# Windowed-attention layers: engine programs reordered, and exponentials taken head by head with the negated maximum as bias

## The reference

```python
for i in range(DEPTH):          # DEPTH = 6, 16 heads of 64, window 32
    x = attn_layer(shift_tokens(x), Wqkv[i], q_scale[i], k_scale[i], Wo[i]) + x
    x = ffn_layer(shift_tokens(x), ln_g[i], ln_b[i], W1[i], b1[i], W2[i], b2[i]) + x
# attn_layer: q, k, v = x @ Wqkv; q, k = l2norm * scale; rotary;
#   sim = q k^T * 8 over the own and the previous window, masked; softmax(sim) @ v; @ Wo
# ffn_layer: a, gate = split(layernorm(x) @ W1 + b1); a * gelu(gate) @ W2 + b2
```

## Time and profile before

| | us |
|---|---|
| median of three runs | 3662.96 |
| profiled execution | 3655.01 |
| its span, first to last instruction | 3653.2 |
| PE busy | 3035.9 (83%) |
| DVE busy | 2316.2 (63%) |
| ACT busy | 1468.4 (40%) |
| POOL busy | 1495.5 (41%) |

### The profile page before, as it was taken

The page is one execution under the profiler, slowest core; times in us unless marked ns, Lnnn a source line. Parts: engine busy times, 40 slices in busy tenths (PEclk is TensorE's granted clock), DMA queues, the critical chain, the costliest instruction groups (busy, mean ns, idle before and its releaser), DMA issues. The chain is left out here.

```text
span 3653.2 us, 94645 instructions
## 1 busy us (share of the span) xinstructions
PE 3035.9 (83%) x39263; PEld 2166.0 (59%) x39263; DVE 2316.2 (63%) x4318; ACT 1468.4 (40%) x2454; POOL 1495.5 (41%) x1462
## 2 busy tenths in 40 slices
PE   4769999999759888888888888888888859888876
PEld 1168888888736555555555555555555535555544
DVE  6832222222149888888888888888888833655622
ACT  3522222222225455555545545545555514444420
POOL 0043333333137556555655555555555502222100
PEclk9977777777769999999999999999999978999975
DMA  0000000000022112212121121121111100000000
GB/s 26 0 6 0 0 0 0 0 0 0 14 92 55 44 37 57 62 48 57 48 62 47 47 73 41 53 54 56 44 45 36 46 27 1 0 0 0 0 9 12
DMA packets 60542, 109.42 MB, mean 30 GB/s; under 512 B 14466, under 2 KB 18580, under 8 KB 59300
## 3 DMA queue, kind: packets, MB, share of 16 engines
q1 hardware_dynamic: 59668, 103.40, 10.2%
q10 hardware_dynamic: 528, 1.05, 0.1%
HBM read 29.43 MB, written 1.05 MB: 8 GB/s over the span
## 5 line engine op out<-in xcount | busy, mean ns | idle before, releaser
L1551 POOL TENSOR_TENSOR l_rot_a<-l_rot_a,l_rot_b 128x512 f32<-128x512 f32 x384 | 487.5, 1271 | 461.6 <-DVE l_rot_b L1366 459.7
L1560 POOL TENSOR_TENSOR l_qk<-l_rot_a,l_rn 128x512 f32<-128x512 f32 x384 | 391.3, 1049 | 235.3 <-DVEq L1407 235.3
L1022 PE MATMUL l_A<-l_wts,l_H 128*128 128x512 f32 x768 | 411.8, 625 | 29.6 <-ACT l_H L1310 21.3
L1360 DVE TENSOR_TENSOR l_rot_a<-l_A,l_tab 128x512 f32<-128x512 f32 x384 | 263.7, 687 | 167.4 <-ACT l_sq L1244 164.0
L1244 ACT ACTIVATE l_sq<-l_A 128x512 f32<-128x512 f32 x384 | 232.0, 604 | 333.1 <-PE l_A L1022 333.1
L1112 PE MATMUL l_T<-ident,l_qk 128*128 128x128 f32 x1536 | 220.3, 287 | 59.7 <-ACT l_qT L1275 59.6
L1366 DVE TENSOR_TENSOR l_rot_b<-l_A,l_tab 128x512 f32<-128x512 f32 x384 | 261.1, 680 | 0.0
L1370 DVE TENSOR_REDUCE l_ss<-l_sq 128x8 f32<-128x512 f32 x384 | 259.3, 675 | 0.0
L1097 PE MATMUL l_O<-l_pT,l_vw 64*64 64x32 f32 x9216 | 198.8, 220 | 72.6 <-ACT l_pT L1250 70.9
L1112 PEld LDWEIGHTS l_T<-ident,l_qk 128*128 128x128 f32 x1536 | 170.6, 145 | 142.3 <-issue 131.8
L1097 PEld LDWEIGHTS l_O<-l_pT,l_vw 64*64 64x64 f32 x9216 | 187.9, 135 | 95.6 <-ACT l_pT L1250 93.6
(11 more groups left out here) (353 smaller groups left out, 6667.6 us busy)
## 6 DMA issues: line engine op xcount, KB each, us to landing
l_vw<-l_vn SPq DMA_DIRECT2D x384, 128.0 KB
l_vw<-l_vn SPq DMA_DIRECT2D x360, 64.0 KB
l_wts<-in_l_wts SPq DMA_DIRECT2D x18, 650.0 KB, 5.1
l_tab<-in_l_tables SPq DMA_DIRECT2D x6, 1024.0 KB, 5.3
l_wts<-in_l_wts SPq DMA_DIRECT2D x6, 635.5 KB, 4.8
a_mask<-in_a_mask SPq DMA_DIRECT2D x1, 1024.0 KB
result<-x SPq DMA_DIRECT2D x1, 1024.0 KB, 5.1
d_w_qkv<-in_d_w_qkv SPq DMA_DIRECT2D x1, 864.0 KB, 4.4
```

What stands on the lines that cost most here:

```text
L1022: pe.matmul(A[j % 2][:], cols(m), w_of(m)[:, C_QKV + 512 * j:C_QKV + 512 * j + 512], start=True, stop=True).then_inc(pq_done, 1)
L1360: dve.tensor_tensor(rot_a[p][:, j, :].rearrange("p (a d) -> p a d", d=DH), src.rearrange("p (a d) -> p a d", d=DH), table[:, a, t:t + 1, : ...
L1551: pool.tensor_tensor(rot_a[m % 2][:, j, :], rot_a[m % 2][:, j, :], rot_b[:, j, :], ALU.add).then_inc(rot_rdy, 1)
L1560: pool.tensor_tensor(qk[:, j, :].rearrange("p (a d) -> p a d", d=DH), rot_a[p][:, j, :].rearrange("p (a d) -> p a d", d=DH), rn[p][:, 8 * ...
```

## The change

In the attention: `soft_shift` keeps the maximum, now negated by the instruction, and loses the subtraction. `exps` reads the scores from `S` and writes `sd`, with one instruction for each of the 16 heads and that head's negated maximum as the bias. `masks` waits for the exponentials instead of the subtraction.

In the feed-forward part: `normed` moves from DVE to ACT as scale and bias, four instructions at the end of the kind 1 slot; DVE computes the bias (`l_shift`) in one small instruction.

In the orders: on PE `turn_norm` goes from the head of its slot to behind `scores`, `narrow` to behind `masks`, and `turn_probs` 1 before `project(n+2, 2)`; ACT follows. On DVE `feed_back` goes behind rope 1, and `add_back` goes before `inverse_roots`. The first step of `inverse_roots` takes a constant instead of the tile `half`.

```diff
--- before.py
+++ after.py
...
@@ -1034,3 +1035,3 @@
             def masks(m):
-                pe.wait_ge(sd_rdy, m)
+                pe.wait_ge(e_rdy, m)
                 for e in range(2):
@@ -1182,4 +1183,2 @@
             for n in range(FIRST_SLOT, LAST_SLOT + 1):
-                if group_at(n, 2) is not None:
-                    turn_norm(n, group_at(n, 2))
                 if group_at(n, 3) is not None:
@@ -1190,4 +1189,2 @@
                     linears(k, 0)
-                if group_at(n, 4) is not None:
-                    narrow(group_at(n, 4))
                 if has(n + 2):
@@ -1196,5 +1193,11 @@
                     masks(n)
+                if group_at(n, 4) is not None:
+                    narrow(group_at(n, 4))
+                if has(n):
                     scores(n, range(HP))
+                if group_at(n, 2) is not None:
+                    turn_norm(n, group_at(n, 2))
                 if has(n - 1):
                     turn_probs(n - 1, 0)
+                    turn_probs(n - 1, 1)
                 if has(n + 2):
@@ -1202,3 +1205,2 @@
                 if has(n - 1):
-                    turn_probs(n - 1, 1)
                     values(n - 1)
@@ -1252,4 +1254,8 @@
             def exps(m):
-                act.wait_ge(sd_rdy, m + 1)
-                act.activation(sd[m % 2][:], sd[m % 2][:], ACT.Exp).then_inc(e_rdy, 1)
+                act.wait_ge(mx_rdy, m + 1)
+                if m >= 2:
+                    act.wait_ge(p_rdy, m - 1)
+                for a in range(HEADS):
+                    last = act.activation(sd[m % 2][:, a, :], S[:, a, :], ACT.Exp, bias=mx[:, a:a + 1])
+                last.then_inc(e_rdy, 1)
 
@@ -1296,2 +1302,10 @@
 
+            def normed(n, k):
+                act.wait_ge(shift_rdy, k + 1)
+                act.wait_ge(xnT_done, k)
+                for i in range(GT):
+                    c = 2 * HEADS + i
+                    last = act.activation(xn[:, i, :], xt[:, i, :], ACT.Identity, scale=rn[n % 2][:, c:c + 1], bias=shift[:, i:i + 1])
+                last.then_inc(xn_rdy, 1)
+
             def gelu(k, i):
@@ -1311,2 +1325,6 @@
             for n in range(FIRST_SLOT, LAST_SLOT + 1):
+                if group_at(n, 3) is not None:
+                    gelu(group_at(n, 3), 2)
+                if has(n + 2):
+                    square(n + 2, 1)
                 if group_at(n, 2) is not None:
@@ -1316,12 +1334,7 @@
                     keep_norm(k)
-                if group_at(n, 3) is not None:
-                    gelu(group_at(n, 3), 2)
-                if has(n + 2):
-                    square(n + 2, 1)
                 if has(n - 1):
                     keep_pT(n - 1, 0)
+                    keep_pT(n - 1, 1)
                 if has(n + 2):
                     square(n + 2, 2)
-                if has(n - 1):
-                    keep_pT(n - 1, 1)
                 if has(n):
@@ -1346,2 +1359,4 @@
                     square(n + 3, 0)
+                if group_at(n, 1) is not None:
+                    normed(n, group_at(n, 1))
 
@@ -1374,8 +1389,4 @@
                 dve.wait_ge(s_done, m + 1)
-                dve.tensor_reduce(mx[:], S[:], AX, ALU.max).then_inc(mx_rdy, 1)
-                dve.wait_ge(mx_rdy, m + 1)
-                if m >= 2:
-                    dve.wait_ge(p_rdy, m - 1)
-                dve.tensor_tensor(sd[m % 2][:], S[:], mx[:].rearrange("p (a o) -> p a o", o=1).to_broadcast([P, HEADS, 2 * WIN]),
-                                  ALU.subtract).then_inc(sd_rdy, 1)
+                dve.wait_ge(e_rdy, m)
+                dve.tensor_reduce(mx[:], S[:], AX, ALU.max, negate=True).then_inc(mx_rdy, 1)
 
@@ -1399,4 +1410,6 @@
                     dve.wait_ge(qk_rdy, 4 * (m - 2) + 4)
+                if group_at(n - 2, 1) is not None:
+                    dve.wait_ge(xn_rdy, group_at(n - 2, 1) + 1)
                 dve.wait_ge(ss_rdy, 4 * m + 4)
-                step(dve.scalar_tensor_tensor(low, low, 1e-24, half[:], ALU.max, ALU.mult), 1)
+                step(dve.tensor_scalar(low, low, 1e-24, -0.5, ALU.max, ALU.mult), 1)
                 step(dve.scalar_tensor_tensor(y.bitcast(I32), low.bitcast(I32), -0.5, magic[:], ALU.mult, ALU.add), 2)
@@ -1420,2 +1433,3 @@
                 dve.wait_ge(st_rdy, GT * k + GT)
+                dve.wait_ge(xn_rdy, k)
                 for i in range(GT):
@@ -1451,7 +1465,3 @@
                 r = rn[n % 2][:, 2 * HEADS:]
-                dve.wait_ge(xnT_done, k)
-                for i in range(GT):
-                    last = dve.scalar_tensor_tensor(xn[:, i, :], xt[:, i, :], mv[:, i, 0:1], r[:, i:i + 1].to_broadcast([P, D]),
-                                                    ALU.subtract, ALU.mult)
-                last.then_inc(xn_rdy, 1)
+                dve.scalar_tensor_tensor(shift[:], mv[:, :, 0], -1.0, r, ALU.mult, ALU.mult).then_inc(shift_rdy, 1)
 
@@ -1517,6 +1526,6 @@
                     product(group_at(n, 3), 0)
-                if group_at(n, 4) is not None:
-                    feed_back(group_at(n, 4))
                 if has(n + 2):
                     rope(n + 2, 1)
+                if group_at(n, 4) is not None:
+                    feed_back(group_at(n, 4))
                 if has(n):
@@ -1529,5 +1538,8 @@
                     rope(n + 2, 3)
+                if has(n - 1):
+                    add_back(n - 1)
+                if has(n + 2):
                     if group_at(n, 1) is not None:
                         dve.wait_ge(var_rdy, group_at(n, 1) + 1)
-                    inverse_roots(n + 2)
+                    inverse_roots(n, n + 2)
                 elif group_at(n, 1) is not None:
@@ -1535,4 +1547,2 @@
                     lone_roots(group_at(n, 1))
-                if has(n - 1):
-                    add_back(n - 1)
                 if group_at(n, 1) is not None:
```

More of the change, by code:

```diff
@@ L887, in local_layers @@
         rn_t = sb("l_rn_t", [P, RN])
-        half = sb("l_half", [P, RN])
         magic = sb("l_magic", [P, RN])
@@ L905, in local_layers @@
         mv = sb("l_mv", [P, GT, 2])
+        shift = sb("l_shift", [P, GT])
         xn = sb("l_xn", [P, GT, D])
@@ L926, in local_layers @@
             "rn_step", "rn_rdy", "qk_rdy", "qkT_done", "qkT_rdy", "kc_rdy"))
-        s_done, mx_rdy, sd_rdy, e_rdy, rs_sum, rs_rdy, p_rdy = (sem("l_" + s) for s in (
-            "s_done", "mx_rdy", "sd_rdy", "e_rdy", "rs_sum", "rs_rdy", "p_rdy"))
+        s_done, mx_rdy, e_rdy, rs_sum, rs_rdy, p_rdy = (sem("l_" + s) for s in (
+            "s_done", "mx_rdy", "e_rdy", "rs_sum", "rs_rdy", "p_rdy"))
         v_done, v_rdy, vw_rdy = (sem("l_" + s) for s in ("v_done", "v_rdy", "vw_rdy"))
@@ L935, in local_layers @@
             "g_done", "gl_rdy", "a_done", "u_rdy", "f_done", "f_rdy", "edge_rdy", "side_rdy"))
+        shift_rdy = sem("l_shift_rdy")
         back_done, back_rdy = sem("l_back_done"), sem("l_back_rdy")
@@ L1388, in sums, with inverse_roots @@
                 dve.reciprocal(rs[:], rs[:]).then_inc(rs_rdy, 1)
-            def inverse_roots(m):
+            def inverse_roots(n, m):
                 low, y, t, base = ss[m % 2][:], rn[m % 2][:], rn_t[:], NEWTON * m
@@ L1495, in _ @@
                 dve.memset(ss[p][:], 1.0)
-            dve.memset(half[:], -0.5)
             dve.memset(magic[:], float(0x5F3759DF - (1 << 30) - (1 << 22)))
@@ L1517, in _ @@
                     product(group_at(n, 3), 0)
+                if has(n + 2):
+                    rope(n + 2, 1)
                 if group_at(n, 4) is not None:
                     feed_back(group_at(n, 4))
-                if has(n + 2):
-                    rope(n + 2, 1)
                 if has(n):
```

## The result

The changed kernel takes 3826.76 us, the median of four runs (3822.58 to 3830.05), against 3665.11 for the kernel before, the median of four runs beside it (with 3662.96 as the median of its first three): a ratio of 1.0435 (95% interval 1.0404 to 1.0466). It is slower, as forecast, and 37 us above the predicted 3790, inside the range of 3695 to 3860. The profiled span grew from 3653.2 to 3820.8 us.

The account below looks back on a forecast made before the run. A loop through DVE, ACT and PE was taken to bound the kernel. 22.5 periods lose 110 us and the first five steps 20: 3655 + 130 = 3785, stated as 3790, range 3695 to 3860.

Parts of the forecast that it names:

- The loop: DVE-ACT-PE chain from one end of `output` (y) to the next: four-slot period of 79.8 us at full clock, from 77.5.
- The sixteen exponentials: On ACT, sixteen 64-column instructions replace one of 1024 columns: 3.42 us from first start to last end, not 1.06.
- `add_back` first: On DVE, `add_back` and then the roots follow the end of `output`: rope 0 starts 3.31 us after it, not 2.01.
- `normed` on ACT: 3.70 us leave DVE, `l_shift` takes 0.8 there; four ACT instructions take 1.5 in all; PE's wait for `l_xn` stays under 2.
- PE's waits for `l_qT`: PE, before `turn_qk` 2, waits 4.8, 2.2, 3.1 and 1.8 us in slot kinds 1, 2, 3 and 0.
- The waits of DVE: DVE waits about 1.6 us at `sums` in most slots and near 1.9 at `add_back` in each slot.
- y to the start of the exponentials: From the end of `output` to the exponentials' start: 9.8, 9.3, 10.9 and 11.4 us in kinds 1, 2, 3, 0.
- The clock: Half clock on PE behind its `l_qT` wait: 2.2 times a period at 1.6 us each, 3.5 in all, making 83.3.
- DVE's load: Rival, 0.07: DVE's busy time sets the pace and falls 7.8 us a period, so the kernel gets faster, 3475 us.
- The quiet clock: Rival, 0.16: PE's clock doesn't fall more often, so the kernel takes 3698 to 3706 us.
- The serial case: Rival, 0.09: small exponentials on ACT don't overlap and take 4.96 us a slot; 146 us on top, 3935.
- No change: Rival, 0.06: an exponential's fixed part is near 0.1 us, not 0.154; a period is 78.2 with kind 1's half clock.

Follow-up runs that it names:

- e3: The changed kernel with `add_back` behind `inverse_roots` again, all else kept: 3663.68 us, 0.9996 of the kernel before.
- e2: The kernel before with only the sixteen exponentials with bias, without the subtraction; orders and `normed` as before: 3791.88 us, 1.0353 of the kernel before.
- e4: The changed kernel with 1 to 4 unused projections on PE in front of `turn_qk` 2: 3733.84 us, 1.0182 of the kernel before.
- e5: The changed kernel with the subtraction and single exponential back and `add_back` behind `inverse_roots`: 3502.34 us, 0.9541 of the kernel before.
- e8: e5 with `project_v` on PE in front of `turn_qk` 2 and 3: 3495.74 us, 0.9528 of the kernel before.

## Why the prediction was right, and where it was short

Point by point, by the prediction's own steps:

- **The loop.** It holds. At full clock the four kinds take 19.9, 19.3, 20.5 and 21.1 us after the change (each mean slot less what its last piece exceeds 4.76, without the last slot of the stack), together 80.8, where 19.4, 18.9, 20.5 and 21.0, together 79.8, were predicted.
- **The sixteen exponentials.** 3.42 predicted, 3.38 measured. The single instruction is longer than thought, 365 ns at the median instead of 310, and the overlap larger by as much: (3.38 - 0.37) / 15 is 0.20 from start to start. The estimate from the Trainium skill's page "ScalarE: Activation LUTs", section "What ACT_TABLE_LOAD costs", was 3.93; the measurement decides. A single one is longer here than the 333 ns that the Trainium skill's figures there make for 64 columns, an estimate from that page, and the overlap is larger than its 93 ns (365 less 200), so that the row of sixteen is cheaper.

```profile
L1259 ACT ACTIVATE l_sd<-l_S,l_mx x1536: 305/365/438, 1089.6 to 3101.8; 128x64 f32<-128x64 f32 x192
```

- **`add_back` first.** Rope 0 starts 3.39 after y, predicted 3.31; e3 shows that this place is worth 163 us in the changed kernel.
- **`normed` on ACT.** The four took 478 ns each, predicted 460; `l_shift` 1.05, predicted 0.8. The wait of PE for `l_xn` was predicted under 2 us and is 2.5 on average (59.8 in 24); the roots, which `l_shift` needs, now start only after y. This is one of the prediction's own signs of being right that failed.
- **PE's waits for `l_qT`.** Predicted 4.8, 2.2, 3.1 and 1.8 in kinds 1, 2, 3 and 0; the timeline of PE has 4.9, 1.7, 2.8 and 1.4 on average.
- **The waits of DVE.** `sums` was to wait about 1.6 and waits 1.9 on average (184.0 in 96). `add_back` was to wait near 1.9 in each slot and waits 3.2 (303.1 in 96). The half clock in front of y, 1.1 us a slot on average, is part of this; the parts were not split.
- **y to the start of the exponentials**, the first undersized term: predicted 9.8, 9.3, 10.9 and 11.4, measured 10.3, 9.7, 10.9 and 11.5. Most of it is in kind 1, and it is a misreading rather than a new cost. The prediction took rope 0 to the maximum, 5.14, from the one slot of the earlier trace rows. That was a short one: over the kernel before the mean of this stretch is 5.75, and after the change it is 5.67. The last step of `moments`, four columns, took 0.32 in that slot (first row) and over 1.2 in ten others of the 24 (second row: the shortest, the median and the longest in ns). Over the four kinds this term is 1.0 a period.

```profile
1653.58 0.32 DVE L1424 TENSOR_SCALAR l_ss<-l_mv 128x4 f32<-128x4 f32 x1
...
L1424 DVE TENSOR_SCALAR l_ss<-l_mv x24: 171/427/1252, 1181.0 to 2961.9; 128x4 f32<-128x4 f32 x24
```

- **The clock**, the second: "2.2 x 1.6 = 3.5" a period, measured 2.4 + 1.1 + 1.0 + 0 = 4.5 in kinds 1, 2, 3, 0 (6.4 being the fall in every slot). In kind 1 the half clock covers `turn_qk` and `project_v` and costs 2.4, not 1.6. In kind 2, 14 of 21 slots pay, not 0.4 of them: there a wait of 1.7 follows PE's wait for `l_xn` in the same slot, 2.2 to 2.4 in each of these, and the prediction counted each wait alone. The 14 that pay waited 1.4 to 2.0 for `l_qT`; of the 7 others six waited 1.0 to 1.2. In e3, where PE waits for `l_xn` in only one of these slots, none of 22 waits of 1.1 to 2.0 at this place costs anything. This speaks for the two waits acting together, but only one of e3's waits is as long as the 2.0 of most that pay, and no run changes one wait alone. Kind 3 has fewer, 9 of 20 instead of 0.7, at about 2.2 each.

The two terms make 2.0 of a period. Over the stack it is 1.8 (85.1 against 83.3), as that last kind 1 slot is 3 us shorter. Times 22.5 periods these are 40 us, less 2 us over the first five steps (17.9 measured, 20 predicted; the first took 15.5, the others 19.4 to 20.4 where 19.4 was predicted). That is the miss in the profiled execution: 168 measured, 130 predicted. The mechanism held piece by piece, so the direction was no luck. The size of the clock's term rests on few slots: the share of slots that fall to half clock was counted on 15 waits, and came out higher in kind 2 and lower in kind 3.

- **The rivals.** DVE's load is refuted: DVE has 242 us less to do and the program is slower; the freed time is in front of `sums` (184.0 us) and `add_back` (303.1). The Trainium skill's page "Perfetto Trace Analysis", section "Optimizing Scalar/DVE Operations", proposes moving work from a saturated DVE to Scalar; e2 moves the subtraction that way from a DVE that is busy for 86% of a period, and costs 3.5%. Whether 86% is saturated that page of the Trainium skill doesn't say; here the busy share didn't decide it. The quiet clock is refuted by the clock itself, and e4 measures what it would have given: at least 93 us. The serial case is out by its 3.38 us. "No change" would have needed a fixed part near 0.1 us an instruction; 0.15 stands.

What the prediction didn't see is how much the rest of the change is worth. It had one number for the whole of kind 2; e5 shows that the other orders with `normed` on ACT take 163 us off, and that the two losing parts put 324 on top.

## What to carry to other kernels

Where two engines are each 86% busy, add up one round between them: if the pieces make the whole period, an instruction counts for its length between waits and not for its load, and work taken off a busy engine is lost if it lengthens the chain. A step that waits for the end of a round (here `add_back`) goes behind everything that the next round needs, however short it is. And a wait on PE is priced twice, as time and as clock: look at every wait with the ones just before it. Unused work in the gap gave 93 us back here (e4); useful work moved into it only moved the gap (e8), so count what the moved matmul itself waits for.

## What the runs showed of the hardware

- **Padding paid.** Ten unused 512-column matmuls a period made the program 2.4% faster (3733.84 against 3826.76), because PE behind them ran at 2.4 GHz and not at 1.2: the granted clock from 1300 to 2700 us rose from 0.93 to 0.98.
- **A short wait can cost the clock.** Waits of up to 1.6 us at `turn_qk` 2 left the clock full in kind 0 (none of 22 slots took over 0.2 us longer); in kind 2, behind another wait of 2.2 to 2.4 us, 14 of 21 waits did cost it, all of them 1.4 to 2.0 long. Waits of 2.5 to 3.0 in kind 3 cost it in 9 of 20, and waits of 4.2 to 5.4 in kind 1 in all.
- **Sixteen small ACT instructions take three times as long as one with the same columns**: 0.20 us from start to start for 64 columns, 0.05 of it the columns. One instruction of 1024 columns took 1.06, so the cut by heads costs 2.3 us on ACT, against the 1.2 us of subtraction it saves on DVE.
- **A tiny DVE instruction can take a microsecond, by waiting for POOL.** The one of `l_shift` has four columns and took from 161 to 1053 ns. In 22 of 24 cases a multiplication of POOL (`l_qk`) had started 10 ns before it, and `l_shift` ended 17 to 19 ns after the end of that one; the first row is two of these multiplications. In the last two cases POOL was idle, and it took 161 and 164 ns. In e3, where it starts later against POOL's work, the median is 164 ns, and each of the longer ones again ends 17 to 19 ns after the multiplication that had begun before it. So it lasted as long as what was left of POOL's instruction.

```profile
2074.22 2.04 POOL L1570 TENSOR_TENSOR l_qk<-l_rot_a,l_rn 128x512 f32<-128x512 f32 x2 [7.08 <-DVEq L1420]
2074.23 1.05 DVE L1466 SCALAR_TENSOR_TENSOR l_shift<-l_mv,l_rn 128x4 f32<-128x4 f32 x1
...
L1466 DVE SCALAR_TENSOR_TENSOR l_shift<-l_mv,l_rn x24: 161/1050/1053, 1221.9 to 3130.3; 128x4 f32<-128x4 f32 x24
```
